# A recurrent layer's norms rebuilt on VectorE's statistics, its first chunk loaded first, and the last chunk's norms moved into the first step of the layers behind it

## Chip, cores and metric

One Trainium2 chip, one of its cores. The metric is the device time of one execution in microseconds (us): the median of three runs of the kernel before is 3591.42 us.

## What is computed

Two blocks follow each other, both with a layer norm in front and a residual sum behind.

```python
x = L0_attn_x                                   # (8, 512, 128), f32
x = x + recurrent(layernorm(x), A, B, C, gamma, beta)
x = x + layers(layernorm(x), ...)               # 6 layers: windowed attention with rotation, then a gated ffn

def recurrent(x, A, B, C, gamma, beta):
    xb = einsum('bsd,ed->sbe', x, B)
    def step(h, xb_t):
        h = tanh(h @ A.T + xb_t)                # 512 steps, one after the other
        return h, h @ C.T
    _, ys = scan(step, zeros, xb)
    out = transpose(ys) + x
    mu, var = mean(out), mean((out - mu) ** 2)
    return (out - mu) * rsqrt(var + 1e-5) * gamma + beta
```

So each token has three norms of 128 values before the layers: one ahead of the recurrence, one behind it (with gamma and beta), and one ahead of the layers.

## The kernel before

Each engine has its own program, and semaphores order them. The 512 tokens of each of the 8 batches are cut into `NC = 8` chunks of 64 tokens; a chunk is a tile of 128 partitions x `TB = 4` rows x 128 values (batch and token are spread over partitions and the four rows).

*The recurrence.* TensorE does a product of 128x128 by 128x8 for each token (line 509), ScalarE its tanh (line 712), and two more products (`keep_warm`) are issued behind each. Between the steps of a chunk other work is put in at fixed tokens: `outputs(c - 1)` at token 3 (h C for the chunk before), `turn_input(c - 1)` at token 38 (transposes of the finished input of the layers, from `lnd`), `turn_xn(c + 1)` at token 54. VectorE does the norms beside it: `normalise(c)` is the norm ahead of the recurrence, `post(c)` adds the chunk's input to h C (line 868), norms it, applies gamma and beta (870, 871), adds the residual (872) and norms again. `layernorm` is a chain of 18 instructions with a wait on the last behind each: sum (93), mean (94), difference (95), square (96), sum (97), variance (98), 11 small ones for the inverse root (63 to 73), product (102).

*The start.* SyncE's queue loads the identity and the mask, A, B, C, gamma, beta, then the 8 chunks of x in two transfers each (line 320), then tables and weights. VectorE first casts identity and mask, then norms chunk 0. TensorE transposes A, B, C, then chunk 0, and starts.

*The end.* Behind the last token TensorE does `outputs(7)`, waits for all of `post(7)`, transposes its result (`turn_input(7)`, line 489); ScalarE copies it into `xa` (`take_input(7)`, line 705), and only then come the layers.

*The layers.* 192 tiles of 128 tokens go through a pipeline written out by hand: `step(s)` on each engine works at tile `A = s` (projection of q and k, line 526; rotation `rope` on VectorE, 896 and 899; squares on ScalarE, 733; their sums on VectorE, 905; the inverse roots, 912 to 920), tile `B = s - 1` (GpSimd scales, 430; TensorE turns, 533; scores, 660 and 667), and so on. Tile 0 needs chunk 0 alone; chunk 7 is first read by tile 28. The same routine `project` is called twice in a step, for q and for k; the second waits until VectorE has read the first and ScalarE has squared it (`q_roped`, `sq_done`).

`ps` is PSUM; `xs` the projection's input, `cosp` and `sinp` the rotated products, `sq` the squares, `ss` their sums, `rr` the inverse roots.

Of the kernel before, what the change touches and what calls it, by code (L numbers as in the profile page):

```python
# [86 lines left out]


def layernorm(eng, step, src, dst, c, t4, bits):

    shape = [P, TB, D]
    mean, var, half, r = (t4[:, i, :] for i in range(4))
# [12 lines left out]
LN_STEPS = 7 + NSTEPS  # L105
# [7 lines left out]
def build(nc, a):  # L113
    with ExitStack() as ctx:  # L114
# [62 lines left out]
        lnc = sq[:, 0, 0:CH].rearrange("p (j d) -> p j d", j=TB)  # L177
        lno = sq[:, 1, 0:CH].rearrange("p (j d) -> p j d", j=TB)
        lnd = sinp[:, 0, 0:CH].rearrange("p (j d) -> p j d", j=TB)
# [3 lines left out]
        gam = sh[:, 0:D]  # L183
        bet = sh[:, D:2 * D]
# [12 lines left out]
        abc_in = sem("abc_in")  # L197
        x_in = [sem(f"x_in{c}") for c in range(NC)]
# [112 lines left out]
        def _(eng):  # L311
            for name, dst in (("ident", ident[:, :]), ("mask", mask_f[:, :])):
                eng.dma_start(dst, a[name]).then_inc(consts_in, 16)
            for i, name in enumerate("ABC"):
                eng.dma_start(abc[:, i, :], a["L0_attn_" + name]).then_inc(abc_in, 16)
            for name, dst in (("L0_attn_gamma", gam), ("L0_attn_beta", bet)):
                eng.dma_start(dst, a[name].rearrange("(o d) -> o d", o=1).to_broadcast([P, D])).then_inc(abc_in, 16)
# [147 lines left out]
        def _(eng):  # L465
            eng.wait_ge(abc_in, 16 * 5)
            eng.wait_ge(consts_in, 32)
# [52 lines left out]
            turn_input(NC - 1)  # L520
# [85 lines left out]
            def step(s):  # L606
                A, B, C, E = s, s - 1, s - 2, s - 3
                if tile(A):
# [3 lines left out]
                    project(A, 0)  # L612
                if tile(C):
                    eng.wait_ge(centered, C + 1)
# [79 lines left out]
        def _(eng):  # L694
# [22 lines left out]
            take_input(NC - 1)  # L717
# [62 lines left out]
            def step(s):  # L780
# [12 lines left out]
                if tile(A):  # L793
                    square(A, 0)
                if tile(C):
# [56 lines left out]
        def _(eng):  # L852
            eng.wait_ge(consts_in, 32)
            eng.tensor_copy(ident_bf[:, :], ident[:, :]).then_inc(tables_ready, 1)
            eng.tensor_copy(mask[:, :], mask_f[:, :]).then_inc(tables_ready, 1)

            def normalise(c):
                after(eng, ln1_turned, c - 1)
                step = Steps(eng, ln1_step, c * LN_STEPS)
                layernorm(eng, step, x1[:, c, :, :], xn_tm[:, c % 2, :, :], lnc, t4, b4[:, :])  # L860
                assert step.n == LN_STEPS

            def post(c):
                row = x1[:, c, :, :]
                eng.wait_ge(hs_turned, c + 1)
                after(eng, post_turned, c)
                step = Steps(eng, post_step, c * POST_STEPS)
                step(eng.tensor_tensor(lno, ps[:, 4, :].rearrange("p (j d) -> p j d", j=TB), xn_tm[:, c % 2, :, :], ALU.add))
                layernorm(eng, step, lno, lnd, lnc, t4, b4[:, :])
# [3 lines left out]
                layernorm(eng, step, row, lnd, lnc, t4, b4[:, :])  # L873
                assert step.n == POST_STEPS

            eng.wait_ge(x_in[0], 32)
            normalise(0)
            for c in range(1, NC):
# [181 lines left out]
```

## Time and profile before

| | |
|---|---|
| median of 3 runs | 3591.42 us (3590.84 to 3592.39) |
| the profiled execution's own time | 3594.22 us |
| its span | 3592.4 us |
| PE busy | 3398.3 us, 95% |
| DVE / ACT / POOL busy | 2724.5 / 2259.3 / 2268.4 us |
| start to the first tanh's product | 19.4 us |
| recurrence | 19.4 to 383.7 us |
| the layers' first projection | 403.80 us |

The span is the profiled stretch; the execution's time is 1.8 us longer. PE is TensorE's matmul, DVE VectorE, ACT ScalarE, POOL GpSimd. TensorE's granted clock is given as a share of its full 2.4 GHz: 0.50 is 1.2 GHz.

### The profile page before, as it was taken

To read this page: it belongs to the slowest core of one execution; us is meant where nothing else is said; L and a number is where in the kernel's file an instruction comes from. 1 tells how busy PE (TensorE), PEld (TensorE's weight loads), DVE (VectorE), ACT (ScalarE), POOL (GpSimd) and SP (SyncE) were. 2 spreads that over 40 slices of the span, in tenths; PEclk is the share of its full clock that TensorE was granted. 3 is DMA by queue.
4 is the path that set the end of the run, shared out by engine and by line. 5 is a ranking of instruction groups with operands and counts; after the bars stand their busy time and mean duration, and the time that the engine had idled before them with its cause. 6 is when DMAs were issued, how large, how long until landed. Compare 5 with 4: busy or idle time off the path is not lost. (4 is left out here: it accounts for less than half of the span.)

```text
span 3592.4 us, 100959 instructions
## 1 busy us (share of the span) xinstructions
PE 3398.3 (95%) x42643; PEld 2179.3 (61%) x42643; DVE 2724.5 (76%) x4175; ACT 2259.3 (63%) x4403; POOL 2268.4 (63%) x1363
## 2 busy tenths in 40 slices
PE   8999699999999999999999999999999999999997
PEld 4555366666666666666666666666666666666664
DVE  3444488888788888788888788787888887888882
ACT  2222266666667767676667666776767666766674
POOL 0000277776777776767777677777676776776762
PEclk9999799999999999999999999999999999999998
DMA  2000000100000100001000001000001000000000
GB/s 69 1 1 1 4 11 11 34 8 11 11 16 9 34 11 11 9 15 34 11 11 8 11 16 34 8 11 10 11 14 34 11 11 8 15 13 16 14 8 13
DMA packets 62279, 52.51 MB, mean 15 GB/s; under 512 B 11526, under 2 KB 59396, under 8 KB 61828
## 3 DMA queue, kind: packets, MB, share of 16 engines
q1 hardware_dynamic: 61828, 46.05, 4.8%
q8 instruction: 338, 5.54, 0.7%
q14 instruction: 113, 0.93, 0.1%
HBM read 43.93 MB, written 2.10 MB: 13 GB/s over the span
## 5 line engine op out<-in xcount | busy, mean ns | idle before, releaser
L440 POOL TENSOR_TENSOR cosp<-cosp,sinp 128x1024 f32<-128x1024 f32 x384 | 908.7, 2366 | 227.5 <-DVE sinp L899 227.4
L430 POOL TENSOR_TENSOR cosp<-cosp,rr 128x1024 f32<-128x1024 f32 x384 | 722.5, 1902 | 487.8 <-DVE rr L920 487.6
L621 PEld LDWEIGHTS ps<-px,w_vo 128*128 128x128 f32 x6144 | 707.0, 192 | 246.1 <-issue 160.9
L621 PE MATMUL ps<-px,w_vo 128*128 128x128 f32 x6144 | 731.6, 278 | 106.2 <-issue 101.9
L526 PE MATMUL ps<-w_qk,xs 128*128 128x512 f32 x1536 | 750.7, 612 | 9.3 <-ACT sq L733 4.5
L896 DVE TENSOR_TENSOR cosp<-ps,tab 128x1024 f32<-128x1024 f32 x384 | 469.8, 1223 | 371.6 <-PE ps L526 371.5
L905 DVE TENSOR_REDUCE ss<-sq 128x16 f32<-128x1024 f32 x384 | 455.4, 1186 | 95.5 <-ACT sq L733 95.5
L733 ACT ACTIVATE sq<-ps 128x1024 f32<-128x1024 f32 x384 | 391.5, 1019 | 215.9 <-DVE sinp L899 215.8
L526 PEld LDWEIGHTS ps<-w_qk,xs 128*128 128x128 f32 x1536 | 263.5, 191 | 342.7 <-issue 341.0
L681 PE MATMUL ps<-pT,xtm 32*128 32x512 f32 x3072 | 458.6, 616 | 9.1 <-DVE pT L971 4.4
L899 DVE TENSOR_TENSOR sinp<-ps,tab 128x1024 f32<-128x1024 f32 x384 | 466.5, 1215 | 0.0
L786 ACT COPY px<-ps 128x512 f32<-128x512 f32 x768 | 393.2, 597 | 58.9 <-PE ps L681 55.1
L533 PEld LDWEIGHTS ps<-ident,cosp 128*128 128x128 f32 x3072 | 355.2, 142 | 116.5 <-issue 102.0
L435 POOL TENSOR_TENSOR pn<-ex,rsum 128x1024 f32<-128x1024 f32 x192 | 365.1, 1902 | 85.6 <-DVE rsum L959 85.5
L533 PE MATMUL ps<-ident,cosp 128*128 128x128 f32 x3072 | 400.4, 274 | 12.2 <-ACT w_vo L802 10.6
L812 ACT COPY kT<-ps 128x512 f32<-128x512 f32 x384 | 206.3, 589 | 284.0 <-PE ps L533 284.0
L667 PEld LDWEIGHTS ps<-kT,qT 64*32 64x32 f32 x24576 | 254.1, 105 | 85.9 <-issue 79.5
L493 PE MATMUL ps<-ident_bf 128*128 128x512 bf16 x1024 | 304.0, 378 | 0.0
L667 PE MATMUL ps<-kT,qT 64*32 64x64 f32 x24576 | 286.1, 225 | 2.9 <-ACT kT L812 1.8
L681 PEld LDWEIGHTS ps<-pT,xtm 32*128 32x128 f32 x3072 | 170.9, 184 | 157.3 <-issue 88.0
L956 DVE TENSOR_REDUCE esum<-ex 128x16 f32<-128x1024 f32 x192 | 232.6, 1212 | 37.1 <-ACT ex L792 37.0
L509 PEld LDWEIGHTS ps<-cosp,qT 128*128 128x128 f32 x1024 | 154.2, 189 | 166.6 <-ACT cosp L712 156.2
(105 smaller groups left out, 4148.0 us busy)
## 6 DMA issues: line engine op xcount, KB each, us to landing
tab<-in_tab SPq DMA_DIRECT2D x96, 128.0 KB, 2.0
qks<-in_scales SPq DMA_DIRECT2D x96, 128.0 KB, 3.2
w_qk<-in_L_ffn_Wqkv SPq DMA_DIRECT2D x12, 512.0 KB, 6.6
w_v<-in_wv_t SPq DMA_DIRECT2D x6, 512.0 KB, 8.5
w_o<-in_L_ffn_Wo SPq DMA_DIRECT2D x6, 512.0 KB, 8.9
x<-in_L_attn_x SPq DMA_DIRECT2D x16, 128.0 KB, 3.5
out<-w_v SPq DMA_DIRECT2D x16, 128.0 KB, 2.4
w<-in_L_ffn_W SPq DMA_DIRECT2D x6, 341.0 KB
```

The costliest lines, as they stand in the source:

```text
L430: eng.tensor_tensor(v, v, rr[:, B % 2, HEADS * i:HEADS * i + HEADS].unsqueeze(2).to_broadcast([P, HEADS, DH]), ALU.mult).then_inc(rot_read ...
L440: eng.tensor_tensor(cosp[:, A % 2, i, :], cosp[:, A % 2, i, :], sinp[:, i, :], ALU.add).then_inc(rot_added, 1)
L526: t = eng.matmul(ps[:, u, :], xs[:, n % ROUND, :], w_qk[:, n // TILES % 2, i, 512 * u:512 * u + 512], start=True, stop=True)
L533: t = eng.transpose(G(k)[:, 128 * m:128 * m + 128], cosp[:, n % 2, i, at:at + 128], ident[:, :])
L621: t = eng.matmul(S0, w_vo[:, i // HP, i % HP, :], px[:, i, :], start=i == 0, stop=i == HEADS - 1)
L667: t = eng.matmul(ps[32 * b:32 * b + 32, 2 + h2, DH * hp:DH * hp + DH], qT[rows, hp, 32 * b:32 * b + 32], kT[rows, B % NG, hp, b, :], start ...
L681: t = eng.matmul(G(b), xtm[rows, C % NG, k, :], pT[rows, :].rearrange("p (h k q) -> p h k q", k=2, q=WIN)[:, :, k, :], start=k == 0, stop= ...
L733: eng.activation(sq[:, i, :], R.rearrange("p a n -> p (a n)"), ACT.Square).then_inc(sq_done, 1)
L786: eng.copy(px[:, :, 32 * b:32 * b + 32], G(b).rearrange("p (h q) -> p h q", q=WIN)).then_inc(px_evac, 1)
L896: eng.tensor_tensor(cosp[:, n % 2, i, :].rearrange("p (h d) -> p h d", d=DH), src, cos, ALU.mult).then_inc(roped, 1)
L899: eng.tensor_tensor(sinp[:, i, :].rearrange("p (h u f) -> p h u f", u=2, f=32), swapped, sin, ALU.mult).then_inc(roped, 1)
L905: eng.tensor_reduce(ss[:, HEADS * i:HEADS * i + HEADS], sq[:, i, :].rearrange("p (h d) -> p h d", d=DH), AX_X, ALU.add).then_inc(ssq_done, 1)
```

## The change

1. `layernorm` uses VectorE's statistics: four `bn_stats` (one for each of the tile's four rows), four `bn_aggr`, one addition of epsilon, the same 11 for the inverse root, and four `tensor_scalar` that subtract the mean and multiply by the root. The four of a kind are issued without a wait between them (`issue`), and one wait stands behind them (`settle`).
2. The queue loads chunk 0 of x first, then identity, A, B, C, the mask, gamma and beta, and the chunks 1 to 7. VectorE norms chunk 0 before it casts identity and mask.
3. `post(7)` is cut in three. Only its sum stays ahead of the layers; `post_norm` stands in step 0 behind the first `rope`, `post_input` behind the second. `turn_input(7)` on TensorE and `take_input(7)` on ScalarE stand in step 1.
4. The buffers `lno`, `lnd`, `gam` and `bet` move into `hh` and `ge`, which the layers use later.

```diff
-def layernorm(eng, step, src, dst, c, t4, bits):
...
-    step(eng.tensor_reduce(mean, src, AX_X, ALU.add))
-    step(eng.tensor_scalar(mean, mean, 1.0 / D, None, ALU.mult))
-    step(eng.tensor_tensor(dst, src, mean.unsqueeze(2).to_broadcast(shape), ALU.subtract))
-    step(eng.tensor_tensor(c, dst, dst, ALU.mult))
-    step(eng.tensor_reduce(var, c, AX_X, ALU.add))
-    step(eng.tensor_scalar(var, var, 1.0 / D, EPS, ALU.mult, ALU.add))
+    def issue(self, ins):
+        ins.then_inc(self.sem, 1)
+        self.n += 1
+
+    def settle(self):
+        self.eng.wait_ge(self.sem, self.base + self.n)
+
+
+def layernorm(eng, step, src, dst, stat, aggr, t4, bits):
+
+    var, half, r = (t4[:, i, :] for i in range(3))
+    for j in range(TB):
+        step.issue(eng.bn_stats(stat[:, j, :], src[:, j, :]))
+    step.settle()
+    for j in range(TB):
+        step.issue(eng.bn_aggr(aggr[:, j, :], stat[:, j, :]))
+    step.settle()
+    step(eng.tensor_scalar(var, aggr[:, :, 1], EPS, None, ALU.add))
     rsqrt(eng, var, bits, half, r, step.sem, step.base + step.n)
...
-    step(eng.tensor_tensor(dst, dst, r.unsqueeze(2).to_broadcast(shape), ALU.mult))
+    for j in range(TB):
+        step.issue(eng.tensor_scalar(dst[:, j, :], src[:, j, :], aggr[:, j, 0:1], r[:, j:j + 1], ALU.subtract, ALU.mult))
+    step.settle()
...
-        lno = sq[:, 1, 0:CH].rearrange("p (j d) -> p j d", j=TB)
-        lnd = sinp[:, 0, 0:CH].rearrange("p (j d) -> p j d", j=TB)
+        lno = hh[:, 0, :].rearrange("p (j d) -> p j d", j=TB)
+        lnd = hh[:, 1, :].rearrange("p (j d) -> p j d", j=TB)
...
+            load_x(0)
+            eng.dma_start(ident[:, :], a["ident"]).then_inc(ident_in, 16)
+            for i, name in enumerate("ABC"):
+                eng.dma_start(abc[:, i, :], a["L0_attn_" + name]).then_inc(abc_in, 16)
+            eng.dma_start(mask_f[:, :], a["mask"]).then_inc(consts_in, 16)
+            for name, dst in (("L0_attn_gamma", gam), ("L0_attn_beta", bet)):
+                eng.dma_start(dst, a[name].rearrange("(o d) -> o d", o=1).to_broadcast([P, D])).then_inc(scale_in, 16)
+            for c in range(1, NC):
+                load_x(c)
...
@@ tensor @@
-            eng.wait_ge(abc_in, 16 * 5)
-            eng.wait_ge(consts_in, 32)
+            eng.wait_ge(abc_in, 16 * 3)
+            eng.wait_ge(ident_in, 16)
...
             outputs(NC - 1)
-            turn_input(NC - 1)
...
+                if s == 1:
+                    turn_input(NC - 1)
+                    eng.wait_ge(x_updated, NC)
...
@@ scalar @@
-            take_input(NC - 1)
...
                 if tile(A):
                     square(A, 0)
+                if s == 1:
+                    take_input(NC - 1)
...
@@ vector @@
-            for c in range(NC):
+            for c in range(NC - 1):
                 if c:
                     post(c - 1)
-                if c < NC - 1:
-                    normalise(c + 1)
-            post(NC - 1)
+                normalise(c + 1)
+            post(NC - 2)
+            last = Steps(eng, post_step, (NC - 1) * POST_STEPS)
+            post_sum(NC - 1, last)
...
                     rope(A, 0)
+                if s == 0:
+                    post_norm(last)
...
                     rope(A, 1)
+                if s == 0:
+                    post_input(NC - 1, last)
```

On TensorE, at the seam between recurrence and layers, this stood before (`qT`, `px`: C and the last chunk's h; `sinp`: the finished input; `w_qk`, `xs`: projections of tiles 0, 0 and 1):

```order
L482 MATMUL ps<-qT,px 128x128 [waits post_step,hs_done]
L482 MATMUL ps<-qT,px 128x128 x3
L489 MATMUL ps<-ident,sinp 128x128 [waits x_updated,post_step]
L489 MATMUL ps<-ident,sinp 128x128 x3
L526 MATMUL ps<-w_qk,xs 128x512 [waits wq_in,xs_ready]
L526 MATMUL ps<-w_qk,xs 128x512
L526 MATMUL ps<-w_qk,xs 128x512 [waits wk_in,sq_done,q_roped]
```

And this stands there now (line 496 is the old 482, 503 the old 489, 539 the old 526, 546 the old 533):

```order
L496 MATMUL ps<-qT,px 128x128 [waits post_step,hs_done]
L496 MATMUL ps<-qT,px 128x128 x3
L539 MATMUL ps<-w_qk,xs 128x512 [waits wq_in,xs_ready]
L539 MATMUL ps<-w_qk,xs 128x512
L539 MATMUL ps<-w_qk,xs 128x512 [waits wk_in,sq_done,q_roped]
L539 MATMUL ps<-w_qk,xs 128x512
L539 MATMUL ps<-w_qk,xs 128x512 [waits sq_done,k_roped,xs_ready]
L539 MATMUL ps<-w_qk,xs 128x512
L503 MATMUL ps<-ident,hh 128x128 [waits x_updated,post_step]
L503 MATMUL ps<-ident,hh 128x128 x3
L546 MATMUL ps<-ident,cosp 128x128 [waits rot_ready,x_updated]
```

The transposes of the last chunk have moved from ahead of the first projection to behind the third, and what follows them now waits for ScalarE's copy (`x_updated`) too.

On VectorE, in step 0, between the rotation of k and the inverse roots, this stands now (924 and 927 are `rope`, 933 the sum of the squares, 940 the first of the inverse roots); the 11 instructions of `rsqrt` are left out of the middle, and the row of 105 is the last ahead of them:

```order
L933 TENSOR_REDUCE ss<-sq 128x16 [waits sq_done,post_step]
L924 TENSOR_TENSOR cosp<-ps,tab 128x1024 [waits k_done]
L927 TENSOR_TENSOR sinp<-ps,tab 128x1024
L887 TENSOR_TENSOR hh<-hh,ge 128x512
L888 TENSOR_TENSOR hh<-hh,ge 128x512 [waits post_step]
L889 TENSOR_TENSOR x<-x,hh 128x512 [waits post_step]
L100 BN_STATS stat<-x 128x6 [waits post_step]
L100 BN_STATS stat<-x 128x6 x3
L103 BN_AGGR aggr<-stat 128x2 [waits post_step]
L103 BN_AGGR aggr<-stat 128x2 x3
L105 TENSOR_SCALAR t<-aggr 128x4 [waits post_step]
```

Before, the sum of k's squares followed the rotation directly; now the rest of chunk 7's work stands between them.

## Rows read from the trace of the kernel before

**Rows 1.** Busy time in two stretches: microseconds (count), then clock, DMA share, GB/s.

```profile
384.91:403.80 18.89, 2.27 (x12) 1.68 (x13) 13.93 (x40) 1.11 (x4) 0.71 (x1) 0.56 0.00 0
500.00:1000.00 500.00, 479.75 (x6527) 317.29 (x6526) 414.27 (x600) 344.47 (x621) 363.11 (x217) 1.00 0.05 14
```

**Rows 2.** Timeline of the start: start us, us, engine, line, op, out<-in.

```profile
4.00 10.63 SPq L320 DMA_DIRECT2D x<-in_L_attn_x  x16
5.08 0.23 DVE L854 CAST ident_bf<-ident 128x128 bf16<-128x128 f32 x1 [5.08 <-DMA ex<-in_mask]
5.22 0.69 DVE L855 CAST mask<-ex 128x1024 bf16<-128x1024 f32 x1
...
8.55 0.90 PE L469 MATMUL ps<-ident,qT 128*128 128x128 f32 x3 [8.55 <-DMA sh<-in_L_attn_beta]
9.45 0.69 DVE L93 TENSOR_REDUCE t<-x 128x4 f32<-128x512 f32 x1 [3.54 <-DMA x<-in_L_attn_x]
...
14.92 0.69 DVE L102 TENSOR_TENSOR cosp<-cosp,t 128x512 f32<-128x512 f32 x1
```

**Rows 3.** Time to landing of x's transfers, and of others (KB each, median us).

```profile
DMA to landing us min/median/max: 2.9/3.5/4.6
```

```profile
tab<-in_tab SPq DMA_DIRECT2D x96, 128.0 KB, 2.0
...
ex<-in_mask SPq DMA_DIRECT2D x1, 512.0 KB, 3.9
```

**Rows 4.** Timeline in the last chunk's recurrence: end of post(6), and TensorE's turn.

```profile
358.68 0.69 DVE L102 TENSOR_TENSOR sinp<-sinp,t 128x512 f32<-128x512 f32 x1
...
366.68 0.60 PE L489 MATMUL ps<-ident,sinp 128*128 128x128 f32 x4
```

**Rows 5.** Timeline of the seam between recurrence and layers.

```profile
384.91 1.16 PE L482 MATMUL ps<-qT,px 128*128 128x128 f32 x8 [0.98 <-POOL px L409]
...
386.89 0.69 DVE L93 TENSOR_REDUCE t<-sq 128x4 f32<-128x512 f32 x1
...
390.19 0.17 DVE L63 TENSOR_SCALAR b<-t 128x4 int32<-128x4 int32 x1
...
392.37 0.69 DVE L102 TENSOR_TENSOR sinp<-sinp,t 128x512 f32<-128x512 f32 x1
...
400.75 0.69 DVE L102 TENSOR_TENSOR sinp<-sinp,t 128x512 f32<-128x512 f32 x1
...
402.64 0.59 ACT L705 COPY xa<-ps 128x512 f32<-128x512 f32 x1 [18.94 <-PE ps L489]
```

```profile
403.80 3.78 PE L526 MATMUL ps<-w_qk,xs 128*128 128x512 f32 x4 [1.19 <-ACT xs L722]
```

**Rows 6.** Timeline of the layers' own use of the statistics, four of each.

```profile
524.46 0.85 DVE L927 BATCH_NORM_STATS2 stat<-ps 128x6 f32<-128x128 f32 x4
525.23 0.35 DVE L931 BATCH_NORM_AGGREGATE aggr<-stat 128x2 f32<-128x6 f32 x4
```

**Rows 7.** Timeline of the layers' first steps.

```profile
418.25 1.22 DVE L905 TENSOR_REDUCE ss<-sq 128x16 f32<-128x1024 f32 x1 [1.09 <-ACT sq L733]
...
421.38 3.76 POOL L430 TENSOR_TENSOR cosp<-cosp,rr 128x1024 f32<-128x1024 f32 x2 [1.80 <-DVE rr L920]
...
421.78 1.23 DVE L896 TENSOR_TENSOR cosp<-ps,tab 128x1024 f32<-128x1024 f32 x1 [0.48 <-PE ps L526]
...
424.17 1.02 ACT L733 ACTIVATE sq<-ps 128x1024 f32<-128x1024 f32 x1 [3.48 <-DVE sinp L899]
...
425.34 3.75 PE L526 MATMUL ps<-w_qk,xs 128*128 128x512 f32 x4 [0.91 <-ACT sq L733]
...
429.13 1.23 DVE L896 TENSOR_TENSOR cosp<-ps,tab 128x1024 f32<-128x1024 f32 x1 [2.68 <-PE ps L526]
```

```profile
432.98 1.98 PE L526 MATMUL ps<-w_qk,xs 128*128 128x512 f32 x4
...
442.70 1.97 PE L533 MATMUL ps<-ident,cosp 128*128 128x128 f32 x8 [4.13 <-ACT w_vo L802]
```

More of the change, by code:

```diff
@@ L182, in build @@
         abcT = qT[:, 3:6, :]
-        gam = sh[:, 0:D]
-        bet = sh[:, D:2 * D]
+        gam = ge[:, 0, 0:D]
+        bet = ge[:, 0, D:2 * D]
         t4 = sb("t4", [P, 4, TB])
@@ L197, in build @@
         abc_in = sem("abc_in")
+        scale_in = sem("scale_in")
+        ident_in = sem("ident_in")
         x_in = [sem(f"x_in{c}") for c in range(NC)]
@@ L311, in _, with load_x @@
         def _(eng):
[L312 to L317, printed above, removed]
-            for c in range(NC):
+            def load_x(c):
                 for r in range(2):
@@ L859, in normalise, with post_sum, post_norm, post_input @@
                 step = Steps(eng, ln1_step, c * LN_STEPS)
-                layernorm(eng, step, x1[:, c, :, :], xn_tm[:, c % 2, :, :], lnc, t4, b4[:, :])
+                layernorm(eng, step, x1[:, c, :, :], xn_tm[:, c % 2, :, :], stat, aggr, t4, b4[:, :])
                 assert step.n == LN_STEPS
-            def post(c):
-                row = x1[:, c, :, :]
+            def post_sum(c, step):
                 eng.wait_ge(hs_turned, c + 1)
                 after(eng, post_turned, c)
-                step = Steps(eng, post_step, c * POST_STEPS)
                 step(eng.tensor_tensor(lno, ps[:, 4, :].rearrange("p (j d) -> p j d", j=TB), xn_tm[:, c % 2, :, :], ALU.add))
-                layernorm(eng, step, lno, lnd, lnc, t4, b4[:, :])
+            def post_norm(step):
+                layernorm(eng, step, lno, lnd, stat, aggr, t4, b4[:, :])
+            def post_input(c, step):
+                row = x1[:, c, :, :]
                 step(eng.tensor_tensor(lnd, lnd, gam.unsqueeze(1).to_broadcast([P, TB, D]), ALU.mult))
@@ L872, in post @@
                 step(eng.tensor_tensor(row, row, lnd, ALU.add))
-                layernorm(eng, step, row, lnd, lnc, t4, b4[:, :])
+                layernorm(eng, step, row, lnd, stat, aggr, t4, b4[:, :])
                 assert step.n == POST_STEPS
+            def post(c):
+                step = Steps(eng, post_step, c * POST_STEPS)
+                post_sum(c, step)
+                post_norm(step)
+                post_input(c, step)
             eng.wait_ge(x_in[0], 32)
             normalise(0)
+            eng.wait_ge(ident_in, 16)
+            eng.tensor_copy(ident_bf[:, :], ident[:, :]).then_inc(tables_ready, 1)
+            eng.wait_ge(consts_in, 16)
+            eng.tensor_copy(mask[:, :], mask_f[:, :]).then_inc(tables_ready, 1)
             for c in range(1, NC):
                 eng.wait_ge(x_in[c], 32)
-            eng.wait_ge(abc_in, 16 * 5)
-            for c in range(NC):
+            eng.wait_ge(scale_in, 32)
+            for c in range(NC - 1):
                 if c:
                     post(c - 1)
-                if c < NC - 1:
-                    normalise(c + 1)
-            post(NC - 1)
+                normalise(c + 1)
+            post(NC - 2)
+            last = Steps(eng, post_step, (NC - 1) * POST_STEPS)
+            post_sum(NC - 1, last)
             def rope(n, i):
```

8 lines of the change are left out of this document (1 added, 7 removed).

## The prediction

> **What bounds the kernel now.** I read the busy times by stretch first. In the layers (500 to 1000 us) TensorE is busy 479.75 of 500 us at full clock [rows 1]; nothing of the change touches that stage, so what it can move lies ahead of it. There are two places where all of TensorE waits: the first 19.4 us, and the seam between recurrence and layers, where it is busy 2.27 us of 18.89 and its clock is granted at 0.56, so mostly at 1.2 GHz [rows 1]. Then the timelines of both. At the start VectorE waits for x until 9.45, and its norm runs to 15.61 (14.92 + 0.69) [rows 2]; TensorE's transposes of A, B, C at 8.55 waited for beta and were done long before that. At the seam the products of the last chunk start at 384.91, and the chain of `post(7)` runs to 401.44, is turned, copied, and lets the first projection go at 403.80 [rows 5]. The recurrence between them is a chain of TensorE and ScalarE which waits for no norm: `post(6)` is over at 359.37, and TensorE asks for it at 366.68 [rows 4]. Everything behind the seam is chained by semaphores, so a microsecond gained at either place should arrive at the end.
>
> **One norm.** Before: 386.89 to 393.06, 6.17 us [rows 5]. After: four statistics 0.85 and four aggregates 0.35, from the layers' own use [rows 6]; the trace has them on PSUM data there, on SBUF data here. Behind each batch a step of 0.03, as between the chained instructions. The addition of epsilon is a small one like line 63, 0.17 + 0.03. The 11 of the inverse root stay, 392.37 - 390.19 = 2.18 [rows 5]. The four `tensor_scalar` of 128x128 do not occur before. The nearest row with one tensor input from SBUF is the cast of 128x128: 0.23, and the next instruction started 0.14 behind it [rows 2], so 3 x 0.14 + 0.23 = 0.65; the dearer bound is that they cost what the statistics do, 0.85 [rows 6]. I take 0.65. Sum: 0.88 + 0.38 + 0.20 + 2.18 + 0.65 = 4.3 us, 1.9 less than before, and 4.1 to 5.0 as bounds.
>
> The Trainium skill ("VectorE: DVE Perf Modes", "Mode 2×_2P") says that an fp32 `tensor_scalar` on SBUF data handles two elements a cycle and a `tensor_tensor` only one. This trace agrees for the cast (1024 elements in 0.69 us, against 1.23 for a product of as many). By its rule the norm is the 4.3 above; were it not to hold for scalars read from a buffer, the norm would be 4.5 and the whole sum 0.6 us smaller.
>
> **The start.** The first transfer of x is issued at about 0.7 instead of 4.00, the second 10.63 / 16 = 0.66 later, at 1.4. Landing: x's 16 transfers took 2.9 to 4.6, all with others in front; a table of the same 128 KB took 2.0 in an empty queue [rows 3]. I take 2.5, so 3.9 (bounds 3.4 and 6.0). The norm then ends at 3.9 + 4.3 = 8.2 instead of 15.61: **7.4 us earlier**, bounds 4.6 and 8.1. Does something else then stand in the way? A, B, C are issued behind x and identity, C at about 3.5, and land by 6.5 even at 2.9; their transposes (0.90) and the copy are over before 8.2. VectorE casts identity and mask behind the norm, and TensorE wants the casts before the recurrence: 0.14 + 0.69 later, 9.1, if the mask is in. The mask is issued at 3.9, took 3.9 [rows 3], so 7.8. TensorE's turn and ScalarE's copy take as long as at the seam, 403.23 - 401.44 = 1.8 [rows 5], until 10.0. So the casts hide behind these with 0.9 to spare; without that cover each late microsecond of the mask counts in full. The other chunks are issued no later than before in any way that matters: the next norm is asked for 50 tokens on.
>
> The Trainium skill ("DMA: Bandwidth & Descriptors", "Anatomy of one DMA") puts about 2.0 us fixed on a transfer and the bytes at 436 GB/s on top. For 128 KB that is an estimate of 2.3, so landing at 3.7 and a start that gains 7.6 in place of 7.4; the trace's rows of x, all above 2.9, carry the load in front of them as well.
>
> **The recurrence.** Its steps gain nothing: the norms beside it are hidden by it already [rows 4].
>
> **The seam.** I follow the new order on the old clock of time (the start's gain comes off at the end).
> - The last chunk's products end at 386.07 [rows 5]. ScalarE no longer stands behind `take_input(7)`, and xs of tile 0 is ready, so the first projection follows at once. TensorE has just been busy; I take the full-clock 1.98 [rows 7], to 388.05; the half-clock one is 3.78 [rows 5].
> - Rotation of q: from 421.78 to 424.17 it took 2.39 [rows 7]. To 390.5.
> - `post_norm`, 4.3: 394.8. It holds up the sum of q's squares, which waits for nothing else: 1.22 [rows 7], to 396.0. The k projection, done meanwhile (391.6 + 3.8 = 395.4), is hidden.
> - Rotation of k, 2.39: 398.4. `post_input`: three operations of 0.72 and a norm, 2.2 + 4.3: 404.9. Sum of k's squares 1.2: 406.1. From there to the end of the inverse roots, where GpSimd starts, 421.38 - 419.47 = 1.9 [rows 7]: 408.0.
> - Step 1: rotation of tile 1's q, to 410.4; its square on ScalarE 1.02, to 411.4; only behind that in ScalarE's order comes `take_input(7)`, another 0.6: 412.0. TensorE has turned the chunk (input ready at 404.9) and now waits for this copy. GpSimd had its first scaling ready at 408.0 + 3.76 / 2 = 409.9, so this is **a new wait of 2 us**, and behind it on TensorE stand the turns of tile 0's q and the k projection of tile 1.
> - The turns at half clock 1.97 [rows 7]: 414.0. The projection 1.98 at full, 3.75 at half clock [rows 7]; as TensorE has been busy for 2 us when it begins, I take the clock to rise in it: 3.0, to 417.0, and VectorE's next rotation starts.
> - Before, that rotation stood at 429.13 [rows 7]. From there the order is the same in both, and VectorE's chain leads. **12.1 us earlier.** Bounds: norms at 5.0 take 1.4, a first projection at half clock 1.8, the last one at half clock 0.8; against that 1.0 if it is at full clock, and up to 1.8 if a later half-clock stretch goes away.
>
> **Sum.** 7.4 + 12.1 = 19.5 us. The profiled execution took 3594.2, so it would take 3574.7; the median of the runs is 2.8 lower, and 3591.4 - 19.5 gives **3571.9 us**.
>
> **The rivals.**
> - *The gain at the seam is partly given back* (chance 0.11): TensorE's clock falls at once, so the first and the last projection run at 1.2 GHz, and the norms cost 5.0. 12.1 - 1.8 - 0.8 - 1.4 = 8.1, and 15.5 in all: 3575.9. For it: at the seam the clock was at 0.56 [rows 1]. Against: that was an idle TensorE.
> - *The start doesn't do what it says* (0.06): the mask or A, B, C land last and hold TensorE, because x, put first, delays them. If the mask landed 7 us after the norm, nothing would be left: 3591.4 - 12.1 = 3579.3. Against: the mask's own 3.9 us.
> - *More* (0.08): half-clock stretches in steps 1 and 2 go away as TensorE's idle time shrinks: two projections at 1.98 instead of 3.7, 3.4 more, 3568.5.
> - *Slower* (0.02): the statistics cost far more on SBUF data. If a norm takes d longer than the old 6.17, the start gains 5.5 - d, the seam 8.4 - 2d, and from d = 3.65 the two norms of `post` pass the 7.3 us to spare [rows 4] and stall the recurrence in each of 7 chunks by 2d - 7.3. It turns at about d = 3.8, a norm of 10.0; at 12 (d = 5.8) the sum is -0.3 - 3.2 + 7 x 4.3 less, 34 us lost, 3625. Against: the same instructions at 0.85 and 0.35 for four [rows 6].
> - *Nothing at all* (0.01), if both gains fall away.
>
> **How the numbers follow.** The forecast keeps 0.72, with a range of its own of 3569 to 3575. The range goes to the rivals at either side: 3567.5 to 3578. A measurement of this kernel tells 0.2%, 7.2 us, from no change. Only the last two rivals, and a piece of the second, stay inside or beyond that: faster 0.96, same 0.02, slower 0.02.
>
> **What the profile would show.** VectorE's first statistics at 3.9 and the end of the first norm at 8.2; a norm of 4.3; the first product of the recurrence near 12.0; a recurrence of 364.3 us as before; TensorE's first projection within 0.2 us of the last chunk's products and 2 us long; TensorE waiting for ScalarE's copy in step 1, about 6 us behind the chunk's turn; k's rotation of tile 1 about 31 us behind the end of those products, where it was 43. I would be wrong if the casts or the mask release the recurrence, if the first projection takes 3.8, if the four `tensor_scalar` take over 1 us, or if steps 2 to 4 give back what steps 0 and 1 gain.

## Result and the profile after

| | before | after |
|---|---|---|
| median of 7 runs each | 3592.04 us (3588.70 to 3592.89) | 3578.11 us (3577.66 to 3580.74) |
| the profiled execution's span | 3592.4 us | 3578.9 us |
| start to the first tanh's product | 19.43 us | 13.40 us |
| from there to the last chunk's products | 365.48 us | 366.29 us |
| from there to the k rotation of tile 1 | 44.22 us | 35.14 us |
| from there to the end of the span | 3163.3 us | 3164.1 us |

The ratio is 0.9965 [0.9953, 0.9976], an interval that leaves out 1: faster, by 13.9 us between the medians. 19.5 were forecast, and the time lies 0.1 us above the upper end of the range (3578). The last four rows of the table give 6.03, -0.81, 9.08 and -0.8: the 13.5 by which the spans differ. So the gain sits where the prediction put it, at the start and at the seam, and each piece is smaller.

The start of the changed kernel, timeline (start us, us, engine, line, op, out<-in, and in brackets the idle time before it and what ended it); it answers to [rows 2]:

```profile
0.72 1.42 SPq L324 DMA_DIRECT2D x<-in_L_attn_x  x2
...
4.78 0.87 DVE L100 BATCH_NORM_STATS2 stat<-x 128x6 f32<-128x128 f32 x4 [4.78 <-DMA x<-in_L_attn_x]
...
8.48 1.11 DVE L110 TENSOR_SCALAR cosp<-x,aggr,t 128x128 f32<-128x128 f32 x4
9.63 0.23 DVE L902 CAST ident_bf<-ident 128x128 bf16<-128x128 f32 x1
...
9.77 0.69 DVE L904 CAST mask<-ex 128x1024 bf16<-128x1024 f32 x1
...
11.53 2.05 PE L518 MATMUL ps<-cosp,qT 128*128 128x512 f32 x2 [0.77 <-ACT cosp L717]
...
13.40 0.41 PE L523 MATMUL ps<-cosp,qT 128*128 128x8 f32 x2
```

x landed at 4.78, not at 3.9. The four `tensor_scalar` of line 110 took 1.11 us, not 0.65. The norm ended at 9.60. The mask's cast (to 10.46) lies under TensorE's turn and ScalarE's copy (to 11.39), as forecast. What TensorE does next, its timeline:

```profile
14.47 0.43 PE L523 MATMUL ps<-cosp,qT 128*128 128x8 f32 x2
...
17.75 0.35 PE L523 MATMUL ps<-cosp,qT 128*128 128x8 f32 x2
...
18.39 0.37 PE L523 MATMUL ps<-cosp,qT 128*128 128x8 f32 x2
...
19.04 0.37 PE L523 MATMUL ps<-cosp,qT 128*128 128x8 f32 x2
```

From 18.39 to 19.04 a step of the recurrence takes 0.655 us. The first four took 1.09 each (13.40, 14.47, ... 17.75). Before there were two such steps (starts at 19.43, 20.49, 21.59, then 22.30). The `keep_warm` products in them are longer too (1.01 for two against 0.59). The granted clock's column reads 1.00 in both stretches, so it does not show this; but the turn just before, four products of 128x128 at 9.65, takes 1.11, and the same at the seam, where the clock is granted at 0.50, takes 1.12. I read the four steps as TensorE at 1.2 GHz.

VectorE at the seam, timeline, answers to [rows 5, 7]:

```profile
382.70 1.23 DVE L924 TENSOR_TENSOR cosp<-ps,tab 128x1024 f32<-128x1024 f32 x1 [1.07 <-PE ps L539]
...
384.98 0.86 DVE L100 BATCH_NORM_STATS2 stat<-hh 128x6 f32<-128x128 f32 x4
...
386.29 1.22 DVE L105 TENSOR_SCALAR t<-aggr 128x4 f32<-128x4 f32 x1
387.54 0.17 DVE L63 TENSOR_SCALAR b<-t 128x4 int32<-128x4 int32 x1
...
390.87 1.22 DVE L933 TENSOR_REDUCE ss<-sq 128x16 f32<-128x1024 f32 x1
392.01 1.22 DVE L924 TENSOR_TENSOR cosp<-ps,tab 128x1024 f32<-128x1024 f32 x1
...
394.27 0.68 DVE L887 TENSOR_TENSOR hh<-hh,ge 128x512 f32<-128x512 f32 x1
394.99 2.72 DVE L888 TENSOR_TENSOR hh<-hh,ge 128x512 f32<-128x512 f32 x1
397.74 0.69 DVE L889 TENSOR_TENSOR x<-x,hh 128x512 f32<-128x512 f32 x1
...
403.32 1.22 DVE L933 TENSOR_REDUCE ss<-sq 128x16 f32<-128x1024 f32 x1
```

Two rows are far too long: line 105, an addition to 4 values in a partition, 1.22 us, and line 888, 2.72 us where its neighbours of the same shape take 0.68 and 0.69. The group of line 105 (duration ns min/median/max):

```profile
L105 DVE TENSOR_SCALAR t<-aggr x24: 170/170/1221, 6.1 to 399.8; 128x4 f32<-128x4 f32 x24
```

GpSimd in the same stretch, timeline:

```profile
385.14 2.34 POOL L454 TENSOR_TENSOR cosp<-cosp,sinp 128x1024 f32<-128x1024 f32 x1 [4.74 <-DVE sinp L927]
394.43 2.72 POOL L454 TENSOR_TENSOR cosp<-cosp,sinp 128x1024 f32<-128x1024 f32 x1 [6.95 <-DVE sinp L927]
406.45 3.76 POOL L444 TENSOR_TENSOR cosp<-cosp,rr 128x1024 f32<-128x1024 f32 x2 [9.29 <-DVE rr L948]
```

Line 454 is GpSimd's addition of the rotated halves, set free by VectorE's rotation. Line 105 ends at 387.51; take away its own 0.17 and it began at 387.34, 0.14 ahead of the recorded end of the first addition (387.48). Line 888 ends at 397.71; take away its own 0.69 and it began at 397.02, 0.13 ahead of the recorded end of the second (397.15). And that second addition was itself 0.4 longer than the usual 2.35: it was issued while line 887 ran, and less 2.35 it began at 394.80, 0.15 ahead of the end of line 887 (394.95). So in all three cases the later one seems to begin about 0.14 before the record of the earlier one ends. This looks like one path into memory that only one of the two engines can hold. The aggregates of line 103 (385.87, 0.38) and most of the statistics of line 100 ran under the first addition in their usual time. The experiments below test this.

TensorE and ScalarE at the seam, timeline, answers to [rows 5, 7]:

```profile
379.69 1.16 PE L496 MATMUL ps<-qT,px 128*128 128x128 f32 x8 [0.98 <-POOL px L423]
380.69 1.88 PE L539 MATMUL ps<-w_qk,xs 128*128 128x512 f32 x4
386.22 3.46 PE L539 MATMUL ps<-w_qk,xs 128*128 128x512 f32 x4 [3.65 <-issue]
```

```profile
409.59 0.58 ACT L721 COPY xa<-ps 128x512 f32<-128x512 f32 x1
410.23 1.97 PE L546 MATMUL ps<-ident,cosp 128*128 128x128 f32 x8 [5.78 <-POOL cosp L444]
411.99 2.80 PE L539 MATMUL ps<-w_qk,xs 128*128 128x512 f32 x4
414.83 1.23 DVE L924 TENSOR_TENSOR cosp<-ps,tab 128x1024 f32<-128x1024 f32 x1 [3.88 <-PE ps L539]
```

The first projection follows the last chunk's products without a gap and at full clock. The new wait is there: the turns of tile 0 start at 410.23, 0.06 behind the end of ScalarE's copy (410.17). The bracket names GpSimd, whose first half of line 444 was done at 408.3; the copy came last. The next projection took 2.80.

### The profile page after: what moved, and what is told of

It reads as the page before. It is cut to its first block and busy times, and to the rows that moved or that the text cites. A ratio compares the mean times of both kernels' runs of the same rounds, so it can differ in the third digit from the quotient of the medians.

```text
span 3578.9 us, 101107 instructions
## 1 busy us (share of the span) xinstructions
PE 3396.3 (95%) x42643; PEld 2181.3 (61%) x42643; DVE 2697.1 (75%) x4319; ACT 2259.1 (63%) x4403; POOL 2268.8 (63%) x1363
```

## The experiments

The times of one kernel spread over 2 to 6 us, and its medians differ between sets of runs (3591.07 to 3592.76 for the kernel before). The stretches of a timeline spread much less for the changed kernel: in its two profiles the recurrence took 366.29 and 366.10, the seam 35.14 and 35.05. So where a part is priced, I read places in the timeline: the first product of the recurrence, the start of the last chunk's products, tile 1's k rotation, and tile 0's last update of `xa` (617.13 before, 602.72 after). Each table row gives the median with its range and the ratio to the kernel before, run on the same chip.

| | median us | ratio [95%] | last chunk's products | tile 0's update |
|---|---|---|---|---|
| order alone | 3589.62 (3586.51 to 3591.08) | 0.9990 [0.9981, 0.9999] | 380.14 | 611.98 |
| norm alone | 3589.51 (3585.68 to 3591.41) | 0.9989 [0.9980, 0.9997] | 383.90 | 612.71 |
| seam alone | 3587.58 (3586.54 to 3590.10) | 0.9987 [0.9978, 0.9995] | 384.60 | 610.84 |
| GpSimd's additions wait | 3574.85 (3573.65 to 3575.53) | 0.9949 [0.9935, 0.9962] | 378.77 | 598.53 |
| two queues | 3578.55 (3576.96 to 3579.66) | 0.9962 [0.9948, 0.9977] | 378.96 | 601.78 |
| warm start | 3577.05 (3574.96 to 3578.50) | 0.9958 [0.9943, 0.9973] | 377.27 | 600.43 |
| second norm late | 3575.40 (3571.61 to 3576.58) | 0.9950 [0.9934, 0.9967] | 379.42 | 599.73 |
| spread | 3571.84 (3569.74 to 3572.98) | 0.9945 [0.9932, 0.9957] | 378.90 | 596.10 |
| all together | 3568.59 (3567.18 to 3569.36) | 0.9936 [0.9924, 0.9949] | 377.02 | 591.40 |
| the changed kernel again | 3579.31 (3576.08 to 3580.53) | 0.9965 [0.9953, 0.9977] | 379.38 | 602.30 |

**The three parts alone.** The kernel before with the new load order and the casts behind the first norm, and nothing else:

```diff
+            load_x(0)
             eng.dma_start(ident[:, :], a["ident"]).then_inc(ident_in, 16)
...
-            for c in range(NC):
+            for c in range(1, NC):
                 load_x(c)
```

> The kernel before with the new load order alone (chunk 0 of x first, its norm ahead of the casts); norm and seam as before. Theory: chunk 0 lands at 4.8 us as in the changed kernel, the old norm of 6.2 ends at 11.0 instead of 15.6, the first product of the recurrence comes at 14.8 instead of 19.4, the seam keeps its 44.2 us from the last chunk's products to tile 1's rotation of k. 4.6 us less, give or take 0.9 for the number of steps of the recurrence that run at the half clock at its start. Rival: landing depends on what is behind in the queue, then another number than 4.8.

x landed at 5.11, and the first product stood at 15.09, 4.34 earlier, all of it by the load. TensorE's timeline of this kernel:

```profile
15.09 0.41 PE L515 MATMUL ps<-cosp,qT 128*128 128x8 f32 x2
...
16.16 0.43 PE L515 MATMUL ps<-cosp,qT 128*128 128x8 f32 x2
...
16.95 0.30 PE L515 MATMUL ps<-cosp,qT 128*128 128x8 f32 x2
```

Only the first step is slow here. The last chunk's products came 4.77 earlier, so 0.43 was won by having one slow step fewer than before.

The kernel before with the new `layernorm` alone:

```diff
-LN_STEPS = 7 + NSTEPS
+LN_STEPS = 3 * TB + 1 + NSTEPS
...
-def layernorm(eng, step, src, dst, c, t4, bits):
+def layernorm(eng, step, src, dst, stat, aggr, t4, bits):
```

> The kernel before with the new norm alone. Theory: a norm costs 4.8 instead of 6.2 wherever GpSimd is idle; the start gains 1.3, the two norms ahead of the layers' first projection 2.7 (first projection 15.0 us behind the last chunk's products start instead of 18.9 less 2.7 = 16.2), the recurrence nothing. 4.0 us less in all. Rival: if the statistics or the four products are slow for themselves at the seam, rows of 1.2 and 2.7 us appear here too.

The first product came 1.14 earlier, and the seam was 3.29 us shorter. The first projection stood 16.18 us behind the last chunk's products (383.90 to 400.08), where it had been 18.89: the two norms in it save 2.71, 1.35 each. No row was stretched: here no work of GpSimd lies beside the two norms.

The changed kernel with the old norm and the old load order, so that only the moved pieces are left:

```diff
-                layernorm(eng, step, lno, lnd, stat, aggr, t4, b4[:, :])
+                layernorm(eng, step, lno, lnd, lnc, t4, b4[:, :])
...
-            load_x(0)
-            eng.dma_start(ident[:, :], a["ident"]).then_inc(ident_in, 16)
+            for name, dst in (("ident", ident[:, :]), ("mask", mask_f[:, :])):
+                eng.dma_start(dst, a[name]).then_inc(consts_in, 16)
```

> The changed kernel with the old norm and the old load order: only the last chunk's norms are spread. Theory: the seam (start of the last chunk's products to tile 1's rotation of k) takes 35.1 + 2 x 1.3 = 37.8 us instead of 44.2, give or take 1 for which operations run into GpSimd's two additions: 6.4 us less in all. The port theory expects VectorE instructions with two SBUF inputs or one in a fast mode to be stretched while GpSimd's additions run. Rival: the norm is hidden behind TensorE here, then 35 us and 9 less.

The stretch from the last chunk's products to tile 1's k rotation took 39.26, 4.96 less than before but 1.5 more than the 37.8 expected. VectorE and GpSimd in this kernel, timelines:

```profile
390.59 1.82 DVE L101 TENSOR_SCALAR t<-t 128x4 f32<-128x4 f32 x1
...
401.84 2.72 DVE L885 TENSOR_TENSOR hh<-hh,ge 128x512 f32<-128x512 f32 x1
```

```profile
390.04 2.35 POOL L447 TENSOR_TENSOR cosp<-cosp,sinp 128x1024 f32<-128x1024 f32 x1 [4.73 <-DVE sinp L920]
401.29 2.72 POOL L447 TENSOR_TENSOR cosp<-cosp,sinp 128x1024 f32<-128x1024 f32 x1 [8.90 <-DVE sinp L920]
```

Both long rows are back with another norm. In the first the victim is line 101, again a small `tensor_scalar` of the norm, and it ends (392.41) as GpSimd ends (392.39). So the long rows belong to the place, not to the statistics. Of the 1.5 us, 0.6 is this row (1.82 where the changed kernel had 1.22), and 0.8 is tile 1's projection, 3.62 in place of 2.80.

At tile 0's update the three parts alone gain 5.15, 4.42 and 6.29, together 15.86; all at once gained 14.41. Of the 1.45 between them, 1.1 lies in the recurrence, which was 0.3 shorter than before in the three kernels taken together and 0.8 longer in the changed one, by the number of its slow first steps.

**The wait between VectorE and GpSimd.** The changed kernel, with GpSimd's two additions of step 0 held back until the norm's stretch is over:

```diff
                         eng.wait_ge(roped, 2 * A + 2)
+                        if s == 0:
+                            eng.wait_ge(post_step, POST_STEPS * (NC - 1) + (1 + LN_STEPS, POST_STEPS)[i])
```

> The changed kernel; in step 0 GpSimd's two additions wait until the norm work beside them is done. Port theory: the addition of epsilon goes from 1.22 to 0.17 us, the product with beta from 2.72 to 0.69, the seam from 35.1 to 32.1 us, and 3.1 us less at the end than the changed kernel (about 3575.0). Rival (these rows are long for another reason, such as the buffers' place): rows and seam stay, 3578.

The timeline of VectorE and GpSimd in this kernel:

```profile
385.37 0.17 DVE L105 TENSOR_SCALAR t<-aggr 128x4 f32<-128x4 f32 x1
...
389.01 2.35 POOL L456 TENSOR_TENSOR cosp<-cosp,sinp 128x1024 f32<-128x1024 f32 x1 [9.53 <-DVE hh L110]
...
393.01 0.69 DVE L890 TENSOR_TENSOR hh<-hh,ge 128x512 f32<-128x512 f32 x1
```

Both rows are at 0.17 and 0.69 again (890 is the old 888), GpSimd's at 2.35. No instruction was removed, and one engine was made to wait longer: that the two engines hold each other up here is shown.

The gain is less direct than the rows. The stretch took 32.98 in place of 35.14, so 2.2 of the 3.1 us had arrived at its end: the first of the inverse roots now ran into GpSimd's late second addition (0.54 in place of 0.19), and tile 1's projection took 3.36 in place of 2.80. Tile 0's update came 219.76 us behind the last chunk's products where it had been 223.03, 3.3 less, so 1.1 more was won behind the stretch, by what I did not trace. That the total lies so near the 3.1 is in part luck. The median is 3.3 below the changed kernel's first one, which belongs to another set of runs.

The Trainium skill ("SBUF — State Buffer", "SBUF: two separate sides") says that VectorE and GpSimd share one pair of ports as an exclusive lock, held for a whole instruction and taken by VectorE for a two-port mode or, against a GpSimd operation that reads SBUF, for two inputs from SBUF. The trace agrees as far as it can: line 105, a `tensor_scalar` with one SBUF input, and line 888, with two, were held up, and `bn_stats`, `bn_aggr` and the rotations from PSUM ran beside GpSimd at 0.86, 0.38 and 1.22. That line 105 was in a two-port mode, and that a port is what the engines share, no row shows.

**The four `tensor_scalar`.** The changed kernel with the constants 0 and 1 in the place of mean and root (so the norm's result is left out: x goes on as it is):

```diff
-        step.issue(eng.tensor_scalar(dst[:, j, :], src[:, j, :], aggr[:, j, 0:1], r[:, j:j + 1], ALU.subtract, ALU.mult))
+        step.issue(eng.tensor_scalar(dst[:, j, :], src[:, j, :], 0.0, 1.0, ALU.subtract, ALU.mult))
```

> The changed kernel with constants (0 and 1) in place of the mean and the root in the four tensor_scalar; so the norms are left out of its output. The prediction's theory (a fast mode that one-input fp32 operations reach, lost through the two scalars read from a buffer): four take 0.65 us instead of 1.11. Rival (the instruction costs the same whatever its scalars): 1.11 stays.

One execution, 3578.16 us. VectorE's timeline:

```profile
8.36 0.64 DVE L110 TENSOR_SCALAR cosp<-x 128x128 f32<-128x128 f32 x4
```

0.64 for the four against 1.11: by the same instruction, shape and buffers, only the scalars differ. My 0.65 was the price of this form. With scalars read from a buffer one takes 0.34 and the next starts 0.26 behind it; with constants it is 0.22 and 0.14. Whether the faster mode is lost or something is added to each instruction, no run here tells.

**The landing of x.** The changed kernel with the second half of chunk 0 issued on ScalarE's queue:

```diff
+            eng.dma_start(x1[FW:2 * FW, 0, :, :],
+                          a["L0_attn_x"].rearrange("(g r) (c t) d -> r c t g d", r=2, t=FW)[1, 0]).then_inc(x_in[0], 16)
             eng.wait_ge(abc_turned, 3)
```

> The changed kernel with the second half of chunk 0 issued by ScalarE's queue. Theory that the issue of the two transfers one after the other (1.42 us of SyncE) sets the landing: first statistics at 4.1 instead of 4.8 to 5.0, 0.7 us less at the start. Rival (first bytes move at about 2 us whatever is issued, and 256 KB take their time): unchanged, 4.8.

```profile
4.22 0.87 DVE L100 BATCH_NORM_STATS2 stat<-x 128x6 f32<-128x128 f32 x4 [4.22 <-DMA x<-in_L_attn_x]
```

x is there at 4.22, 0.56 earlier; the first product at 12.85, and the median (3578.55) is not to be told from the changed kernel's. It had four slow steps as well. In the other profiles with this load order on one queue x landed at 4.65 to 5.11, and in the last kernel below, on two queues again, at 4.45. So of the 0.9 us that the landing was late, 0.2 to 0.6 hung on the second half being issued behind the first on one queue.

The changed kernel with the identity issued ahead of chunk 0:

```diff
-            load_x(0)
             eng.dma_start(ident[:, :], a["ident"]).then_inc(ident_in, 16)
+            load_x(0)
```

> The changed kernel with the identity ahead of chunk 0 in the queue. Theory that a transfer of x takes longer before its first bytes move than the identity does (bytes moved from 1.5 us on with the identity first, from 2.0 us with x first): x lands at 4.8 to 5.0 all the same, though issued 0.47 later. Rival (x's landing counts from its issue): 5.2 to 5.5.

One execution, 3578.3 us. x was issued 0.45 later, at 1.17, and landed at 5.01. The changed kernel, with chunk 0 in front, landed it at 4.78 and in a second profile at 4.65; but two other kernels with chunk 0 in front landed it at 5.02 (GpSimd's additions wait) and 5.11 (order alone). So 5.01 lies inside what the same order gives, and one profile does not tell the two theories apart.

**The slow first steps.** The changed kernel with 23 products of zeros for TensorE, which has nothing to do there, ahead of the recurrence:

```diff
+            eng.wait_ge(warm_set, 1)
+            warm_up(10)
...
+            warm_up(10)
             turn_xn(0)
+            warm_up(3)
             eng.wait_ge(abc_out, 1)
```

> The changed kernel with 23 more products of a zeroed 128x128 by 512 on TensorE, ahead of its first waits and around the turn of chunk 0. Theory: the recurrence starts at full clock: the turn takes 0.6 instead of 1.11, the first large product 1.0 instead of 2.05, and none of the first steps takes 1.09 (four did, 1.7 us in all); the last chunk's products start about 3 us earlier than the 379.7 of the changed kernel. Rival (the products stand in the way of the waits on TensorE): the start moves later by as much as they overrun, up to 2 us.

TensorE's timeline:

```profile
9.58 0.66 PE L498 MATMUL ps<-ident,cosp 128*128 128x128 f32 x4 [0.81 <-DVE cosp L110]
...
12.77 0.30 PE L534 MATMUL ps<-cosp,qT 128*128 128x8 f32 x2
...
13.36 0.37 PE L534 MATMUL ps<-cosp,qT 128*128 128x8 f32 x2
```

No slow step is left, the turn takes 0.66 in place of 1.11, and the last chunk's products start at 377.27 in place of 379.69: 2.4 us, where about 3 were expected. 0.6 of it is turn and products (the pair of large products took 1.95 in place of 2.05, so my halving of it was wrong), 1.8 is steps. The recurrence took 364.50. The transfers that run at this time can't be the cause of the slow steps: they moved 235 GB/s during the four slow steps of the changed kernel (13.40 to 17.75) and 249 GB/s here (12.77 to 15.00). The profiled executions' spans differ by 2.2, the medians by only 1.1, within the spread of the runs.

**The second norm out of step 0.** The changed kernel with `post_input` in step 2 and the turn and copy of chunk 7 in step 3:

```diff
-                if s == 0:
+                if s == 2:
                     post_input(NC - 1, last)
...
-                if s == 1:
+                if s == 3:
                     take_input(NC - 1)
```

> The changed kernel with post_input in step 2 ahead of the rotation of k, where VectorE idles 6.2 us, and chunk 7 turned and copied in step 3. Theory: step 1 no longer waits for ScalarE's copy and step 0 is 7.7 us shorter; in step 2 some 1 to 4 us come back, as GpSimd is busy there and blocks VectorE's small operations. From the last chunk's products to tile 0's last update 217 to 220 us instead of 223.0, and a median of 3572 to 3575. Rival (the delay only moves, since VectorE's work is the chain): 223 and 3578.

The median, 3575.40, and tile 0's update, 220.31 behind the last chunk's products, both lie just above what was expected. The k rotation of tile 1 stood at 405.90, 26.48 behind the last chunk's products (35.14 in the changed kernel). But 8.7 us gained there became 2.7 at tile 0's update (220.31 against 223.03), because step 2 paid:

```profile
417.76 1.90 POOL L449 TENSOR_TENSOR pn<-ex,rsum 128x1024 f32<-128x1024 f32 x1
418.64 1.57 DVE L889 TENSOR_TENSOR hh<-hh,ge 128x512 f32<-128x512 f32 x1
...
419.62 2.79 POOL L454 TENSOR_TENSOR cosp<-cosp,sinp 128x1024 f32<-128x1024 f32 x1
420.24 2.72 DVE L890 TENSOR_TENSOR hh<-hh,ge 128x512 f32<-128x512 f32 x1
```

Lines 889 and 890 are the two products with gamma and beta; they cost 2.9 us more than their 1.38, again beside GpSimd, and the k rotation of step 2 started at 428.58, about 4.6 us behind the projection that it reads.

So the next kernel gives those three operations to GpSimd itself, between its own additions in step 0, holds the first of these until `post_norm` is over, and leaves only the norm to step 2:

```diff
+                        if s == 0 and i == 0:
+                            eng.wait_ge(post_step, POST_STEPS * (NC - 1) + 1 + LN_STEPS)
...
+                            eng.tensor_tensor(lnd, lnd, gam.unsqueeze(1).to_broadcast([P, TB, D]), ALU.mult).then_inc(post_step, 1)
...
+                            eng.tensor_tensor(row, row, lnd, ALU.add).then_inc(post_step, 1)
```

> The kernel of e7 with two more edits: GpSimd's first addition waits for post_norm, and GpSimd itself does gamma, beta and the residual of chunk 7 between its two additions of step 0; VectorE keeps only the last norm, in step 2. Port theory and the theory that VectorE's chain is the seam: the epsilon row is 0.17 us, step 2's 4.8 us lie under the 5 to 6 us for which VectorE waits there, from the start of the last chunk's products to tile 0's last update 214.6 us instead of 220.3 (e7) and 223.0 (changed kernel), and a median near 3570. Rival (GpSimd's three operations delay the scalings behind them, or TensorE's clock sets step 2): 218 or more.

3571.84 us, 7.5 below the changed kernel run beside it (3579.31, below) and 6.3 below its first median. Tile 0's update came 217.20 us behind the last chunk's products, 5.8 less than in the changed kernel; I had expected 214.6. Two small rows were caught once more, one of the inverse roots in step 0, whose usual duration is 0.19, and one of the norm in step 2:

```profile
395.36 2.34 POOL L456 TENSOR_TENSOR cosp<-cosp,sinp 128x1024 f32<-128x1024 f32 x1
395.56 2.19 DVE L952 SCALAR_TENSOR_TENSOR rhalf<-rguess 128x32 f32<-128x32 f32 x1 [0.74 <-ACT rguess L805]
...
419.51 2.35 POOL L456 TENSOR_TENSOR cosp<-cosp,sinp 128x1024 f32<-128x1024 f32 x1
419.84 2.05 DVE L105 TENSOR_SCALAR t<-aggr 128x4 f32<-128x4 f32 x1
```

The first is new: the three operations given to GpSimd push its second addition back until it meets the inverse roots. Together the two rows cost VectorE 3.9 us.

**All together.** This one with the two queues and a warm start of 21 products:

```diff
+            warm_up(10)
...
+            warm_up(8)
             turn_xn(0)
+            warm_up(3)
```

> e9 with chunk 0's second half on ScalarE's queue and TensorE kept busy at the start (e6 and e8). If the three gains add up: start of the last chunk's products at 376.8 (379.7 less 0.5 and 2.4), 214.6 from there, median near 3567. If they meet in one place (the casts or the mask now hold the recurrence): 377.5 or later.

3568.59 us, 10.7 below the changed kernel run beside it and 22.5 below the runs of the kernel before (3591.07): it beats both. The last chunk's products start at 377.02 (376.8 expected), and tile 0's update comes 214.38 behind them. But the same two rows are long here as well (2.18 and 2.04), so the 214.6 was met for another reason than the one expected. From the last chunk's products on this program is the same as the one with the spread alone, and yet it is 2.8 us shorter: 0.75 of it before tile 1's k rotation, where the projection took 2.55 in place of 3.30. Between different kernels of which each has one profile, a difference of 2 to 3 us at tile 0's update is therefore not a price by itself. For the changed kernel's own program behind the recurrence, five profiles gave 222.8 to 223.2.

**The changed kernel again**, beside the last three:

> The changed kernel once more, beside e9 and e10. All theories: 3578 us. Theory that the recurrence's first slow steps and the drain depend on where TensorE's clock rises and not on the code: the number of steps of 1.09 us at its start differs from the four of its first profile, and with it the start of the last chunk's products (379.7 then) by 0.44 a step.

3579.31 us, ratio 0.9965 as at first. x landed at 4.65, and the stretch at the seam was 35.05: the sizes above are not those of one odd execution. There were four slow steps again (1.09, 1.10, 1.09, 0.83), so the theory that their number would differ did not come true here.

## Why the prediction was right in kind and wrong in size

The time lies outside the stated range. The places and the order of events were right; the step that failed most is the seam's sum, which priced "three operations of 0.72" and the norm's "0.17 + 0.03" as if GpSimd did nothing beside them. They cost 3.1 us more. Landing, the `tensor_scalar`, the slow first steps and the end of the run make up the rest.

**The start: 7.4 forecast, 6.03 measured.** The working was right (x first, the casts hidden, the recurrence released by ScalarE's copy). Two terms failed. "Landing: ... I take 2.5, so 3.9": it was 4.78, inside the bounds. I had taken the 2.0 of a table in an empty queue as the nearest row, and x's own fastest transfer, 2.9, was nearer. The Trainium skill's figures ("DMA: Bandwidth & Descriptors", "Anatomy of one DMA"), which its section fits to transfers issued by GpSimd and not by SyncE as here, an estimate of a landing at 3.7, were further off still. "3 x 0.14 + 0.23 = 0.65" for the `tensor_scalar`: it was 1.11, more than even the bound of 0.85. I named this as a sign of error, and the run with constants shows why: the cast was a row of the wrong form. The prediction had doubted this very form, at 0.2 us a norm; it was 0.46. By the rule of the Trainium skill ("VectorE: DVE Perf Modes", "Mode 2×_2P") an fp32 `tensor_scalar` handles two elements a cycle; the trace agrees with the price built on it for constants (0.64), and not for scalars from a buffer (1.11). In the seam both norms carry this 0.46 as well.

**The recurrence: 0 forecast, 0.81 lost.** "Its steps gain nothing" was right, but the steps at its beginning can cost more. Four ran as slowly as at 1.2 GHz, two before. The warm start, which changes hardly anything but what TensorE did before, removes them: it is TensorE's speed, worth 2.4 us with the turn and products ahead of them. Why there are one, two or four is open: kernels with an equal start had between one and four, and the changed kernel had four both times.

**The seam: 12.1 forecast, 9.1 measured.** Against the forecast's own list, with 5.22 us (the gain until there) added to the times after (the end of a row is read as the start of what follows it at once):

| end of | forecast | measured | late by | new in this row |
|---|---|---|---|---|
| q rotation | 390.5 | 390.20 | -0.3 | -0.3 |
| `post_norm` | 394.8 | 396.09 | 1.3 | 1.6 |
| k rotation | 398.4 | 399.49 | 1.1 | -0.2 |
| the three operations | 400.6 | 403.68 | 3.1 | 2.0 |
| `post_input` | 404.9 | 408.54 | 3.6 | 0.6 |
| the inverse roots | 408.0 | 411.67 | 3.7 | 0.0 |
| ScalarE's copy | 412.0 | 415.39 | 3.4 | -0.3 |
| tile 1's projection | 417.0 | 420.05 | 3.05 | -0.35 |

The steps held to a few tenths, the full-clock first projection, the "new wait" for the copy and the 3.0 for the last projection (2.80) among them. What failed is the term "three operations of 0.72" and the norm's small addition of "0.17 + 0.03": 2.03 and 1.05 us more, because GpSimd's addition lay beside them. Holding GpSimd back brought both rows to their usual length. I had costed each row by its own duration in a place where GpSimd was idle, and in the recurrence it was. That step 0 has GpSimd working beside VectorE was in the order; I did not ask what the two share. The rival "the gain is partly given back" had the right sign and nearly the right time (3575.9), for a reason that was largely wrong: its norms at 5.0 came near for the second (4.82), the first took 5.85 with its wait, and the clock of the first projection did not fall (1.88 us, granted at 1.00).

**Behind the seam.** The difference of the two traces stays: 14.41 us at tile 0's update (617.13 and 602.72), 14.46 at the one at 3410.86 (3396.40), 14.38 at 3539.55 (3525.17). Steps 2 to 4 gave nothing back. Then 0.8 is lost between two updates in the drain, 3539.55 to 3568.86 before and 3525.17 to 3555.30 after. TensorE there, timelines, before:

```profile
3544.59 3.84 PE L621 MATMUL ps<-px,w_vo 128*128 128x128 f32 x32 [2.15 <-ACT px L786]
...
3557.64 3.75 PE L568 MATMUL ps<-xf,w 128*128 128x512 f32 x4 [0.98 <-DVE w_v L945]
```

and after:

```profile
3530.22 5.44 PE L637 MATMUL ps<-px,w_vo 128*128 128x128 f32 x32 [2.15 <-ACT px L801]
...
3545.33 1.96 PE L581 MATMUL ps<-xf,w 128*128 128x512 f32 x4 [0.98 <-ACT xr L755]
```

The same groups run partly at half clock in both, but not the same ones: 3.84 has become 5.44 and 3.75 has become 1.96. This stretch took 28.10 us in the kernel with the order alone and 30.1 to 30.2 in the kernels with the seam alone, the norm alone and GpSimd's wait, so it is a variation that goes with where the clock falls; what fixes it I did not find. It is 0.8 of the missing 6.0.

**The sum of what was missing**, against the spans: landing 0.9, the norm at the start 0.5, slow steps 0.8, the two norms at the seam 0.9, the port 3.1, drain 0.8, and 1.1 the other way (0.3, 0.2, 0.3 and 0.35 in the table): 5.9 of 19.5 - 13.5 = 6.0.

## What to carry to other kernels

- A duration from a trace is the price of an instruction in its company. Before work is moved on VectorE, look at what GpSimd does at the new place: a `tensor_scalar`, or an operation on two SBUF tensors, can wait there for nearly a whole GpSimd instruction (2.03 us here, beside one of 2.35), and the profile books that as busy time, not as a wait. The sign to look for is one row far above the median of its own group.
- Price a new instruction by a row with the same kind of operands: constants and scalars from a buffer differ by a factor of 1.7 here.
- Where a chain alternates between engines, making the engine with time to spare wait, or giving it the operation, can be the faster order: 3.3 us at tile 0's update by a wait alone, and 5.8 with the spread. But an operation that is moved can push the next collision elsewhere: the spread made a new one of 2.0 us.

## What the runs showed of the hardware

- A small VectorE operation of 0.17 us took 1.22, 1.82 and 2.05 in three kernels, and ended each time 0.02 to 0.03 us behind GpSimd's addition. GpSimd in its turn was held by a VectorE operation that had begun before it: 2.72 in place of 2.35. Without GpSimd's work beside them the same rows took 0.17 and 0.69.
- Four `tensor_scalar` of 128x128: 1.11 us with scalars from a buffer, 0.64 with constants. Four `bn_stats` and four `bn_aggr` take nearly the same on SBUF data (0.87 and 0.38) as on PSUM data [rows 6].
- Steps of 1.09 us in place of 0.655 stand at the start of the recurrence, one to four of them from kernel to kernel, while TensorE's granted clock is recorded as 1.00. The four transposes ahead of them took 1.11, as they do at a recorded 0.50 (1.12). Products of zeros ahead of them removed both (0.66 and 0.65, and no slow step) in two kernels.
- With 128 KB each on an otherwise empty queue, two halves of x issued at 0.72 and 0.7 later were there at 4.65 to 5.11 (seven profiles); on two queues both were there at 4.22 and 4.45 (two profiles).
